# A 36-step task table of an attention and gate kernel put in another order

## The reference

```python
xn = _layernorm(x, axis=-1)
qkv = xn @ W_attn + b_attn              # q, k turned by rope, 16 heads of 16
att = softmax(causal(q @ k.T * 0.25))
s = (att @ v) @ W_proj + b_proj
gate, up = xn @ wg.T, xn @ wu.T         # 768 wide; weights are integers / 127
g = _silu((_silu(gate) * up) @ wd.T)
out = x + s * g
```

## Time and profile before

| | |
|---|---|
| median of 3 runs | 1216.95 us (1214.07 to 1217.84) |
| the profiled execution | 1217.21 us, its span 1215.5 us |
| mean granted TensorE clock | 0.991 |
| TensorE busy | 1126.6 us (93%) |
| VectorE busy | 1007.0 us (83%) |
| ScalarE busy | 890.8 us (73%) |
| GpSimd busy | 770.5 us (63%) |
| chain that ended last | PE 55%, DVE 14%, POOL 14%, ACT 6%, issue 6%, DMA 3%, SyncE's queue 2% |

### The profile page before, as it was taken

One profiled execution on the slowest core, in us unless ns is written; L12 is line 12 of the kernel. 1 busy time (PEld: TensorE's weight loads), 2 busy tenths in 40 slices (PEclk: granted clock), 3 DMA queues, 4 the chain that ended last, 5 costly groups with the idle time before them and its releaser, 6 DMA issues.

```text
span 1215.5 us, 27634 instructions
## 1 busy us (share of the span) xinstructions
PE 1126.6 (93%) x9484; PEld 454.6 (37%) x9484; DVE 1007.0 (83%) x3092; ACT 890.8 (73%) x1708; POOL 770.5 (63%) x942
## 2 busy tenths in 40 slices
PE   3779999999999999999999999999999999999996
PEld 2223333434334343434334243433434343343433
DVE  6689989988989888888899878898898987989822
ACT  4458777777877778778787777777787786878774
POOL 3536546496836948289564867469492894747672
PEclk9989999999999999999999999999999999999999
DMA  6160041503342151611525024331515115240201
GB/s 175 61 162 11 11 125 63 133 25 99 71 142 62 27 142 33 172 29 35 144 72 134 11 72 108 111 95 28 142 33 171 31 32 146 71 97 15 61 2 53
DMA packets 71281, 97.51 MB, mean 80 GB/s; under 512 B 18398, under 2 KB 44388, under 8 KB 71140
## 3 DMA queue, kind: packets, MB, share of 16 engines
q1 hardware_dynamic: 71072, 95.73, 28.8%
q10 hardware_dynamic: 68, 0.01, 0.0%
HBM read 52.76 MB, written 34.47 MB: 72 GB/s over the span
## 4 chain that ended last, share of the span: by engine, by line
PE 55%; DVE 14%; POOL 14%; ACT 6%; issue 6%; DMA 3%; SPq 2%; POOLq 0%; DVEq 0%; ACTq 0%
PE ring L931 27%; PE acc L922 12%; PE st L871 8%; PE ring L898 6%; DVE ring L1293 4%; POOL xn L579 4%; POOL pexp L1597 3%; DVE mx_s L1297 3%; POOL hf L1627 2%; DMA q_st<-mT 2%; ACT pexp L1127 2%; SPq L640 2%; DVE ga L1357 1%; DVE ln L1320 1%; ACT parts L1169 1%
## 5 line engine op out<-in xcount | busy, mean ns | idle before, releaser
L1127 ACT ACTIVATE pexp<-st 128x512 f32<-128x512 f32 x1152 | 623.6, 598 | 141.3 <-PE st L871 138.6
L1293 DVE CUSTOM_DVE_ANT_0 ring<-ring,tri 128x512 f32<-128x512 f32 (+3 forms) x1024 | 470.5, 522 | 36.6 <-PE ring L898 35.6
L1597 POOL TENSOR_SCALAR_AFFINE_SELECT pexp<-pexp 128x512 f32<-128x512 f32 x256 | 158.0, 635 | 347.2 <-ACT pexp L1127 254.0
L1297 DVE TENSOR_REDUCE mx_s<-ring 128x1 f32<-128x512 f32 x512 | 326.3, 681 | 42.7 <-PE ring L898 41.1
L922 PE MATMUL acc<-pexp,v_pad 128*17 128x512 f32 (+3 forms) x3072 | 303.7, 490 | 12.5 <-POOL pexp L1597 10.2
L898 PE MATMUL ring<-k_st,q_st 56*128 56x512 f16 (+4 forms) x1536 | 239.7, 327 | 20.7 <-DVE g L1365 11.0
L871 PE MATMUL st<-q_st,k_st 58*128 58x512 f16 (+3 forms) x1536 | 235.1, 332 | 13.2 <-DMA q_st<-mT 6.6
L871 PEld LDWEIGHTS st<-q_st,k_st 58*128 58x128 f16 x1536 | 61.9, 93 | 288.3 <-ACT pexp L1127 184.5
L1293 DVE DVE_READ_ACCUMULATOR2_ANT mx_s<- 128x1 f32 x1024 | 145.2, 142 | 0.0
L1627 POOL TENSOR_TENSOR hf<-ga,ups 128x512 f32<-128x512 f32 x96 | 121.9, 1274 | 6.8 <-DVE ga L1357 5.6
L922 PEld LDWEIGHTS acc<-pexp,v_pad 128*17 128x17 f32 x3072 | 61.4, 96 | 148.7 <-issue 119.4
(11 more groups left out here) (152 smaller groups left out, 1330.0 us busy)
## 6 DMA issues: line engine op xcount, KB each, us to landing
parts_scratch<-parts SPq DMA_DIRECT2D x32, 512.0 KB, 2.9
q_st<-parts_scratch SPq DMA_DIRECT2D x62, 192.0 KB, 3.8
k_st<-parts_scratch SPq DMA_DIRECT2D x62, 192.0 KB, 4.5
parts_scratch<-parts SPq DMA_DIRECT2D x32, 256.0 KB, 3.6
xo<-in_x SPq DMA_DIRECT2D x32, 256.0 KB, 3.4
out<-xo SPq DMA_DIRECT2D x32, 256.0 KB, 2.2
xn<-in_x SPq DMA_DIRECT2D x7, 1024.0 KB, 7.3
yn<-yT SPq DMA_DIRECT2D x224, 32.0 KB
```

The lines of the kernel that those rows point to most:

```text
L1127: nc.scalar.activation(pexp[:, GH * (n % NSET) + j, :], st[:, (GH * n + j) % NST, :], ACT.Exp, scale=1.0 / (QK_SCALE * np.sqrt(D))).then_i ...
L1293: top_ = nc.vector.tensor_tensor_reduce(out=src, in0=src, in1=tri[:, CH - w:CH], scale=1.0, scalar=NEG, op0=ALU.add, op1=ALU.max, accum_ou ...
L1297: top_ = nc.vector.reduce_max(dst, src, AX.X)
L1597: nc.gpsimd.affine_select(out=t, in_=t, compare_op=ALU.is_ge, fill=0.0, base=0, pattern=[[0, GH], [1, P]], channel_multiplier=-1).then_inc ...
```

## The change

`ITEMS` and `TASKS` are written in another order; no task and no kind of item is added or dropped. Some lags of GpSimd and SyncE are other numbers. x is loaded for the batch after next, in the second step behind the last TX, in place of the next batch at step 0; the first such load moves to the prologue. The rows of maxima of a group leave in two transfers, one for each part with both sides (rows 64 partitions apart) in it, in place of four; the counts that wait for them follow.

```diff
-ITEMS = ('BF', 'EA', 'FF', 'FF', 'AE', 'AF', 'EA', 'EF', 'BF')
+ITEMS = ('AE', 'FF', 'AF', 'FF', 'BA', 'AF', 'EE', 'EF', 'BF')
...
 TASKS = {
-    0: [("DN", 1, 2), ("YS", 3, 0), ("YS", 3, 1)],
-    1: [("XC", 0), ("UPG", 0, 0)],
-    2: [("V", 0, 1), ("LNS", 0)],
-    3: [("XC", 1), ("YG", 1), ("DN", 1, 3)],
-    4: [("YR", 1), ("LNS", 1), ("UPG", 0, 1), ("UPU", 0, 0)],
-    5: [("LNS", 2), ("UPU", 0, 1), ("YB", 1), ("YC", 1), ("V", 1, 1), ("LNS", 3)],
-    6: [("LNR",), ("V", 1, 0)],
-    7: [("UPG", 0, 2), ("YN", 1, 0), ("MT", 1), ("YS", 0, 0), ("YN", 1, 1)],
-    8: [("UPU", 0, 2)],
-    9: [("LNA", 1), ("UPG", 0, 3)],
-    10: [("UPU", 0, 3), ("LNA", 2)],
-    11: [("LNA", 5), ("UPG", 0, 4)],
-    12: [("FP", 0)],
-    13: [("UPU", 0, 4)],
-    14: [("YS", 0, 1), ("UPG", 0, 5), ("UPU", 0, 5)],
-    15: [("LNA", 6), ("LNA", 3), ("FP", 1), ("LNA", 7), ("FP", 2), ("LNA", 4), ("LNA", 0)],
+    0: [("YS", 3, 0), ("YS", 3, 1), ("XC", 0)],
+    1: [("DN", 1, 2)],
+    2: [("LNS", 0), ("XC", 1), ("V", 0, 1)],
+    3: [("DN", 1, 3)],
+    4: [("LNS", 1), ("YG", 1), ("UPG", 0, 0), ("UPU", 0, 0), ("YR", 1)],
+    5: [("LNS", 2), ("UPG", 0, 1), ("UPU", 0, 1), ("LNS", 3), ("YB", 1), ("YC", 1), ("V", 1, 1)],
+    6: [("V", 1, 0), ("LNR",)],
+    7: [("YS", 0, 0), ("YN", 1, 0), ("YN", 1, 1), ("MT", 1)],
+    8: [("UPG", 0, 2), ("UPG", 0, 3), ("UPU", 0, 2)],
+    10: [("UPU", 0, 3), ("LNA", 7)],
+    11: [("UPG", 0, 4)],
+    12: [("FP", 0), ("YS", 0, 1)],
+    13: [("UPU", 0, 4), ("LNA", 2), ("YS", 1, 0)],
+    14: [("UPG", 0, 5), ("LNA", 4), ("UPU", 0, 5), ("LNA", 5)],
+    15: [("FP", 1), ("LNA", 3), ("LNA", 6), ("LNA", 1), ("LNA", 0), ("FP", 2)],
     16: [("UPG", 1, 0), ("MT", 2)],
-    17: [("YS", 1, 0), ("TX", 0, 1), ("TX", 0, 0), ("TX", 1, 1), ("UPG", 1, 1)],
-    18: [("DN", 0, 0)],
-    19: [("YS", 1, 1), ("TX", 1, 0), ("QK", 0, 1, 1), ("DN", 0, 1)],
-    20: [("DN", 0, 2), ("QK", 0, 0, 1), ("YG", 0), ("QK", 0, 0, 0), ("QK", 0, 1, 0)],
+    17: [("TX", 0, 1), ("TX", 1, 1), ("TX", 1, 0), ("UPG", 1, 1)],
+    18: [("QK", 0, 0, 1), ("QK", 0, 1, 1), ("DN", 0, 0)],
+    19: [("TX", 0, 0), ("YS", 1, 1), ("DN", 0, 1)],
+    20: [("YG", 0), ("QK", 0, 0, 0), ("QK", 0, 1, 0), ("DN", 0, 2)],
     21: [("DN", 0, 3)],
-    22: [("YR", 0), ("UPU", 1, 0), ("UPU", 1, 1)],
+    22: [("UPU", 1, 0), ("YR", 0), ("UPU", 1, 1)],
     23: [("UPG", 1, 2)],
-    24: [("YB", 0), ("QK", 1, 1, 0), ("YC", 0), ("UPU", 1, 2)],
-    25: [("FP", 3), ("MT", 3)],
-    26: [("UPG", 1, 3), ("UPU", 1, 3)],
-    27: [("YS", 2, 0), ("YN", 0, 0), ("UPG", 1, 4)],
-    28: [("YS", 2, 1), ("UPU", 1, 4)],
+    24: [("QK", 1, 1, 0), ("YB", 0), ("YC", 0), ("UPU", 1, 2)],
+    25: [("UPG", 1, 3), ("YN", 0, 0), ("MT", 3)],
+    26: [("UPG", 1, 4), ("FP", 3)],
+    27: [("UPU", 1, 3)],
+    28: [("YS", 2, 0), ("YS", 2, 1), ("UPU", 1, 4)],
     29: [("UPG", 1, 5)],
-    30: [("YN", 0, 1), ("UPU", 1, 5)],
-    31: [("QK", 1, 1, 1), ("QK", 1, 0, 0)],
+    30: [("QK", 1, 0, 0), ("UPU", 1, 5)],
+    31: [("QK", 1, 1, 1)],
     32: [("QK", 1, 0, 1)],
-    33: [("DN", 1, 0), ("DN", 1, 1)],
-    34: [("MT", 0)],
+    33: [("DN", 1, 0)],
+    34: [("YN", 0, 1), ("DN", 1, 1), ("MT", 0)],
     35: [("V", 0, 0)],
 }
 SLOTS = GROUPS * STEPS
+TX_LAST = [t for slot in sorted(TASKS) for t in TASKS[slot] if t[0] == "TX"][-1]
+LOAD_X = [slot for slot in TASKS if TX_LAST in TASKS[slot]][0] + 2
...
-    "gpsimd": {"LNR": 2, "LNA": 0, "XC": 1, "UPU": 2, "HI": 4, "LO": 4, "FP": 2, "FP_G": 2, "FP_X": 4, "YN": 1, "YH": 1, "YL": 2},
-    "sync": {"QK": 2, "MT": 0, "FP": 5, "YS": 0, "YG": 0, "YB": 0, "YC": 1},
+    "gpsimd": {"LNR": 2, "LNA": 0, "XC": 0, "UPU": 3, "HI": 4, "LO": 5, "FP": 3, "FP_G": 3, "FP_X": 4, "YN": 1, "YH": 1, "YL": 2},
+    "sync": {"QK": 5, "MT": 0, "FP": 4, "YS": 1, "YG": 2, "YB": 1, "YC": 1},
...
-        def rows_of_maxima(eng, g, sides):
-            for a in sides:
-                for part in range(2):
-                    row = SIDE * a + MAXROW + part
-                    first = 2 * TT * a
-                    eng.dma_start(q_st[row:row + 1, g, :, :].rearrange("o p (t n) -> o (p t) n", t=TT),
-                                  mT[first:first + 2 * TT, part, :]).then_inc(mrow_in[g], 16)
+        def rows_of_maxima(eng, g, halves):
+            for part in halves:
+                row = MAXROW + part
+                eng.dma_start(q_st[row:row + SIDE + 1:SIDE, g, :, :].rearrange("a p (t n) -> a (p t) n", t=TT),
+                              mT[:, part, :]).then_inc(mrow_in[g], 16)
...
                 rows_of_maxima(sp, 0, (0,))
+                wait_ready(sp, "pro", 0, PRO_IN[-1])
+                stand(sp, sp_stand)
+                load_x(1)
...
-                            if kind != "last":
-
-                                wait_ready(sp, *body_before(kind, i), ("TX", 1, 0))
-                                stand(sp, sp_stand)
-                                load_x(i + 1)
...
                             task(kind, i, t)
+                        if half == 0 and slot == LOAD_X and kind != "last" and i + 2 < B:
+
+                            wait_ready(sp, kind, i, TX_LAST)
+                            stand(sp, sp_stand)
+                            load_x(i + 2)
...
-                    pe.wait_ge(mrow_in[g], 16 * GH * (i + 1))
+                    pe.wait_ge(mrow_in[g], 16 * 2 * (i + 1))
...
-                        act.wait_ge(mrow_in[(t[1] - 1) % GROUPS], 16 * GH * (i + 1))
+                        act.wait_ge(mrow_in[(t[1] - 1) % GROUPS], 16 * 2 * (i + 1))
```

## The result

The changed kernel takes 1220.7 us (median of 20 runs, 1215.1 to 1225.8) against 1215.6 (20 runs, 1211.4 to 1222.3) for the kernel before: a ratio of 1.0041, 95% interval 1.0026 to 1.0057. It is slower by 0.4%. The prediction said 1202, 0.74 for faster, and left 1221 to a rival, x that stands in the way. The profiled execution took 1218.98 us, its span 1217.2; the mean granted clock went from 0.991 to 0.982.

The account below looks back on a forecast made before the run. TensorE was taken as the bound, busy 135.5 of 142 us in a middle batch; only its waits could shrink. Terms of 23.9 us won and 9 lost gave 15 won, 1217.2 to 1202, range 1187 to 1219.

Parts of the forecast that it names:

- x stands in the way: Rival: late stores make TensorE wait 3 us at step 24 in five batches, plus 1.7 clock; 23.5 lost, 1221; chance 0.14.
- x two batches ahead: Load issued in step 21 before the stores of q and k: k's stacks late at step 24, 4 us lost.
- Masks in steps 10 to 12: GpSimd's masks come earlier, with no normalisation before the first: all 9.4 us of TensorE's waits gone; bounds 0 and 11.
- the reason given for the transposes: Step 17: UPU 4 and 5's products and subtractions now follow GpSimd's last normalisation, so transposes should not wait; 0.5 us won.
- Step 20: Both engines take QK and DN in one order, so the gate product's wait goes: 8.5 of 9.4 us won.
- Rows of maxima: Two transfers in place of four land 1.2 us earlier: 4 us won; bounds 5.8 won, 3.5 lost.
- the rival of late rows: Rows land twice today's 1.7 us after issue: 3.5 us lost in place of 4 won, 1209; chance 0.11.
- Steps 0 and 9 without a task: No TensorE task there saves turns between matmuls of different row count: 1.5 us won; bounds 0 and 3.
- Masks in steps 28 to 30: YN (0,0) moves earlier and waits for the inverses, delaying GpSimd's masks behind it: 5 us lost in six batches.
- x two ahead, nothing won directly: Today's load at step 0 makes nobody wait, so loading earlier wins nothing by itself.
- SyncE stopped in steps 28 to 34: Rival: a move of y waits for YN (0,1), holding SyncE's queue; at 4 us per batch 34 lost, 1236; chance 0.13.

## Why the prediction was wrong

The step that failed is *x two batches ahead*, the term "I take 0.8 in five batches": 4 us lost where the five middle waits came to 19.1, the first batch's to 2.0 and the clock took about 11 by estimate; moving x away was worth 29. The mechanism was named there, and as the rival *x stands in the way* (3 us in five batches, with the clock's 1.7, 1221). That the rival's number came out is partly luck: x cost more than its 23.5 (the mean of the five waits is 3.8, and the first batch waited too), and the rest won more than the sum had. Four things made the term too small.
- *The arrival.* k's stacks were forecast to land between 307.9 and 310.2 and TensorE to come at 307.9. In the second batch TensorE came at 306.15 (309.28 - 3.13), 1.75 us earlier: it was 5.8 us ahead of the kernel before there, and not the 4 taken. The landing fell inside its range, TensorE went on at 309.28, but with luck: x was issued 1.0 us earlier than forecast (294.79, not 295.8), and the delay behind it was about as long as the upper bound had it. The term took a third of its own bound, 0.8 of 2.3, while the sum counted the gains that open the wait in full.
- *The spread of the batches.* One batch stood for five. In the third a store of the output landed after 3.7 us, not 2.2, the stacks followed the stores after 9.1 us, not 7.7, and the wait was 5.07. The late store could be read beforehand: in the kernel before the load behind it was issued 3.95 us after it in the third batch (430.77 to 434.72) and 2.2 in the second (287.66 to 289.88).
- *The first batch* was left out because it has no output to store. It loads x in front of the same stores, and waited 2.0 us.
- *The clock* stood only in the rival. Four of the five middle waits were followed by 0.50.

The other terms:
- *Masks in steps 10 to 12*, 9.4 gone: right in the changed kernel (no wait there; the 4.0 left stand in steps 28 to 30), and so is the reason given for the transposes. But it is not a term that can be added: alone with its lags it was worth 0.3 us (1213.8 against 1214.1). Step 20 took 2.5 us of it back; the rest is open.
- *Step 20*, 8.5: right in sign and place, 11.5 measured alone.
- *Rows of maxima*, 4 won: 5.3 measured alone; the rival of late rows falls, with 2.1 us from the first issue to the last record of the transfers.
- *Steps 0 and 9 without a task*, 1.5 won: not seen. The waits on ScalarE went from 3.4 to 8.2 us, and with the steps filled again the time was 1188.9 against 1191.4. What the turns between matmuls of different row count are worth stays open.
- *Masks in steps 28 to 30*, 5 lost: 4.0 us in two batches (1.53 and 0.54, 1.40 and 0.55), about right.
- *x two ahead, nothing won directly*: wrong for the new order, in which x at step 0 costs 19.9 us of waits in step 3.
- *SyncE stopped in steps 28 to 34*: not seen. The second move of group 2 was issued at 492.06, against 491.3 to 491.9 forecast for GpSimd, the rows at 496.18 against 495.39 in the earlier trace rows, and TensorE waited 0.2 us for them in all.

Without x's term the sum was 23.9 - 5 = 18.9 us won; with x behind the stacks 23.4 were (1214.8 to 1191.4). So order, lags and transfers together did what was said of them, a little more, and x's place turned the sign. Term by term that is not shown: step 20 and the two transfers alone are 13.3 of it, and the other 10 were not taken apart.

## What to carry to other kernels

A load that nobody waits for has a price at the place where it is issued: the transfers behind it in the queue land later (here by about 4 us behind 1 MB), and a store that is read back passes that on. Price such a wait with the arrival that your own gains bring forward, in the batch whose queue runs latest, and count the clock behind it. And before gains at two places on one engine are added up, ask whether the second waits for what the first wins: here 5.8 us of waits for the masks went, and the time fell by 0.3 (from 2.9 less to 1.0 more).

## What had not been expected of the hardware

The clock did not follow the length of the wait alone. After 2.01 us of waiting in the first batch it was granted at 0.50 from 169.5 to 172.9, after 2.76 us in the fourth batch it stayed at 1.00, in the run with x at step 0 a wait of 2.98 us was followed by 0.50 (653.9 to 657.3) and one of 3.00, up to 225.1, was not, and in the kernel with the normalisations behind the masks it fell after two waits at the transposes of 1.54 and 0.55. What tells these apart, the runs do not show.
